# Layer statistics of a graph-attention stage moved into the feed-forward steps, with reordered hand-overs in the attention step

## What is computed

```python
# end of the first layer
h2 = _layernorm(hidden, g2, b2)
hidden = hidden + gelu(h2 @ Wf1 + bf1) @ Wf2 + bf2

# second layer: graph_attention with 8 heads, then with one
attn_in = layer_norm(x, g1, b1)
h = einsum('bnd,dhk->bhnk', attn_in, W.reshape(D, H, Dh))
s = einsum('bhnk,hk->bhn', h, a_src)
t = einsum('bhnk,hk->bhn', h, a_dst)
e = leaky_relu(s[:, :, :, None] + t[:, :, None, :], 0.2) + bias[:, None, :, :]
attn = einsum('bhij,bhjk->bhik', softmax(e, axis=-1), h) + x
```

## Time and profile before

| | |
|---|---|
| median of 3 runs | 1096.09 us (1095.07 to 1099.65) |
| profiled execution, its own time | 1097.07 us |
| its span in the trace | 1095.2 us |
| busy: PE, DVE, ACT, POOL | 1043.2, 799.9, 710.2, 405.0 us |
| mean granted clock of PE | 0.989 of full speed |

### The profile page before, as it was taken

How to read it: one execution, slowest core, us unless ns; L and a number is a source line. 1 busy time by engine, 2 the same in 40 slices (tenths; PEclk the granted TensorE clock), 3 DMA queues, 4 the chain that set the end, 5 groups by cost and what they waited for, 6 DMA issues and landing times.

```text
span 1095.2 us, 39179 instructions
## 1 busy us (share of the span) xinstructions
PE 1043.2 (95%) x15924; PEld 915.1 (84%) x15924; DVE 799.9 (73%) x1921; ACT 710.2 (65%) x1718; POOL 405.0 (37%) x642
## 2 busy tenths in 40 slices
PE   5999999999999989999999999999989999979997
PEld 5888888888888868889988998898878888868886
DVE  4577777777777777865656565655678989858996
ACT  2777767777767754555455545555678888847774
POOL 3531121121111104332113211312367888877773
PEclk9999999999999999999999999999989999988999
DMA  9221111221110002110011001110000100001222
GB/s 239 55 46 42 41 41 41 58 62 41 41 41 12 12 2 59 27 32 21 21 28 29 23 21 28 31 40 1 22 23 19 29 19 19 13 3 59 78 78 98
DMA packets 82476, 43.67 MB, mean 40 GB/s; under 512 B 42912, under 2 KB 77984, under 8 KB 82336
## 3 DMA queue, kind: packets, MB, share of 16 engines
q1 hardware_dynamic: 78016, 41.44, 13.9%
q10 hardware_dynamic: 4320, 0.28, 0.3%
HBM read 21.25 MB, written 12.58 MB: 31 GB/s over the span
## 4 chain that ended last, share of the span: by engine, by line
PE 83%; DVE 5%; issue 4%; POOL 3%; ACT 2%; SPq 1%; DMA 1%; POOLq 0%; DVEq 0%; ACTq 0%
PE BK L1344 8%; PE BK L1346 8%; PE BK L1345 8%; PE BK L1473 6%; PE BK L1447 5%; PE BK L1560 5%; PE BK L1561 5%; PE BK L1562 5%; PE BK L1459 4%; PE BK L1440 3%; PE BK L1360 3%; PE BK L1369 3%; PE BK L1607 3%; PE BK L1361 2%; PE BK L1362 2%
## 5 line engine op out<-in xcount | busy, mean ns | idle before, releaser
L1192 ACT ACTIVATE gf<-BK,bcol 128x512 f32<-128x512 f32 x128 | 88.2, 689 | 160.0 <-PE BK L1346 146.5
L965 POOL TENSOR_TENSOR ve<-mv,eps_l 128x4 f32<-128x4 f32 x64 | 18.2, 284 | 438.1 <-DVE mv L314 419.4
L1108 ACT ACTIVATE e_sb<-BK,nmx 128x128 f32<-128x128 f32 x512 | 142.1, 408 | 28.3 <-DVE nmx L501 28.3
L597 DVE TENSOR_TENSOR gl<-gf,gh 128x512 fp32r<-128x512 f32 x128 | 100.8, 790 | 68.4 <-ACT gh L1193 66.6
L1560 PE MATMUL BK<-wf_hi,gh 128*128 128x256 f32 x512 | 142.7, 279 | 1.8 <-DVE gl L597 1.8
L1561 PE MATMUL BK<-wf_hi,gl 128*128 128x256 f32 x512 | 141.8, 277 | 0.0
L1562 PE MATMUL BK<-wf_lo,gh 128*128 128x256 f32 x512 | 141.7, 277 | 0.0
L507 DVE TENSOR_TENSOR pt_sb<-BK,ft 128x512 f32<-128x512 f32 x128 | 85.2, 687 | 59.3 <-PE BK L1447 57.8
L1128 ACT ACTIVATE xn<-x_all,neg_mr,rstd 128x256 f32<-128x256 f32 (+1 forms) x188 | 103.6, 610 | 4.7 <-POOL neg_mr L974 4.4
L1344 PE MATMUL BK<-xh,wf_hi 128*128 128x512 f32 x256 | 99.9, 390 | 1.4 <-DVE xl L341 0.8
L1346 PE MATMUL BK<-xh,wf_lo 128*128 128x512 f32 x256 | 100.9, 394 | 0.0
(11 more groups left out here) (207 smaller groups left out, 2760.8 us busy)
## 6 DMA issues: line engine op xcount, KB each, us to landing
x_all<-in_x_dram SPq DMA_DIRECT2D x16, 512.0 KB, 4.7
out_dram<-y SPq DMA_DIRECT2D x16, 512.0 KB, 2.9
xn<-tb_ln SPq DMA_DIRECT2D x240, 32.0 KB, 1.9
adj_in<-in_adj_dram SPq DMA_DIRECT2D x64, 64.0 KB, 3.6
adj_kept<-adj_tr SPq DMA_DIRECT2D x16, 256.0 KB, 2.3
adj_in<-adj_kept SPq DMA_DIRECT2D x16, 256.0 KB, 2.6
s_wf<-in_L_gnn_Wf_dram SPq DMA_DIRECT2D x2, 1024.0 KB, 7.2
s_w<-in_L_gnn_W_dram SPq DMA_DIRECT2D x2, 256.0 KB, 2.9
```

The source lines that it names most:

```text
L597: dve.tensor_tensor(gl[:, f, :], gf[f % 2][:], gh[:, f, :].bitcast(F32), ALU.subtract).then_inc(b_gl, 1)
L1108: e = act.activation(e_sb[:, j, :], LE[:, r, q, :], ACT.Exp, bias=nmx[:, j:j + 1], scale=1.0)
```

## The change

Three things are moved.

1. The statistics of the multi-head stage's layer norm are no longer made in that stage. New tiles hold mean, reciprocal deviation and shift of all 64 graphs. In feed-forward step i (1 to 15) DVE makes the four bn_stats of chunk i-1 after `gl` 4 (`layer_stats`) and the aggregates after `gl` 5 (`layer_aggr`), and POOL makes deviation and shift (`layer_scale`). Chunk 15 follows in multi-head steps 0 and 1. `far_stats`, `aggr` and POOL's deviations remain in multi-head steps 13 to 15 and 14 to 15, for the single-head stage. The last feed-forward step's own statistics for chunks 0, 1 and 2 go.
2. On PE the values of graph 0 stand right after the row scores, ahead of `c_av` and of the second ratios.
3. On ACT `gt_out` and `row_exps` stand ahead of the two `c_out_copy`; on DVE `row_limits` stands after `c_scale` 4 and `c_recip` after it, ahead of `c_scale` 5.

The core of the diff; the new tiles, the semaphores and the new counts of the shared ones are left out:

```diff
@@ -312,6 +324,24 @@
+def layer_stats(i):
+    wait_for(dve, cs_mv, i * G)
+    for g in range(G):
+        dve.bn_stats(cs_raw[:, g, :], xs(i, g)).then_inc(cs_st, 1)
+
+def layer_aggr(i):
+    dve.wait_ge(cs_st, (i + 1) * G)
+    for g in range(G):
+        dve.bn_aggr(cs_mean[:, i * G + g, :], cs_raw[:, g, :]).then_inc(cs_mv, 1)
+
+def layer_normalise(i):
+    dve.wait_ge(cs_rs, i + 1)
+    dve.wait_ge(ln_t, (i + CC) * KT)
+    for g in range(G):
+        n = i * G + g
+        dve.tensor_scalar(xn[:, g, :], xs(i, g), cs_mean[:, n, 0:1], cs_rstd[:, n:n + 1],
+                          ALU.subtract, ALU.mult).then_inc(ln_xn, 1)
@@ -587,45 +617,37 @@
 def b_step(i, half, par):
     final = isinstance(i, int) and i == NC - 1
-    c = CC if final else CB + 1 if i == 0 else i + CB + 2
+    c = CB + 1 if i == 0 else i + CB + 2
     for f in range(FT):
-        if f == 1 and i != NC - 2:
+        if f == 1 and i < NC - 2:
             dve.wait_ge(ln_st, (c + 1) * G)
         if f == 6 and i == 0:
             dve.wait_ge(ln_st, (CB + 3) * G)
         dve.wait_ge(b_gh, i * FT + f + 1)
         dve.tensor_tensor(gl[:, f, :], gf[f % 2][:], gh[:, f, :].bitcast(F32), ALU.subtract).then_inc(b_gl, 1)
-        if f == 0:
-            dve.wait_ge(*((b_x, G) if final else (a_x, (i + 2) * G)))
+        if f == 0 and i < NC - 2:
+            dve.wait_ge(a_x, (i + 2) * G)
             for g in range(G):
-                if i != NC - 2:
-                    stats(c, c % NC, g)
-        if f == 1 and i != NC - 2:
+                stats(c, c % NC, g)
+        if f == 1 and i < NC - 2:
             aggr(c)
+        if f == 4 and i > 0:
+            dve.wait_ge(b_x, i * G)
+            layer_stats(i - 1)
+        if f == 5 and i > 0:
+            layer_aggr(i - 1)
         if final and f == 2:
             setup_constants()
-        if f == 3 and (i == 0 or final):
+        if f == 3 and i == 0:
             normalise(c, c % NC)
-            if i == 0:
-                block_turn(c)
+            block_turn(c)
+        if f == 3 and final:
+            layer_normalise(0)
         if f == 5 and i == 0:
             for g in range(G):
                 stats(CB + 2, 2, g)
         if f == 6 and i == 0:
             aggr(CB + 2)
-        if final and f == 5:
-            dve.wait_ge(b_x, 3 * G)
-            dve.wait_ge(ln_mv, (CC + 1) * G)
-            for g in range(G):
-                stats(CC + 1, 1, g)
-        if final and f == 6:
-            dve.wait_ge(ln_st, (CC + 2) * G)
-            dve.wait_ge(ln_xn, (CC + 1) * G)
-            aggr(CC + 1)
-        if final and f == 7:
-            dve.wait_ge(ln_mv, (CC + 2) * G)
-            for g in range(G):
-                stats(CC + 2, 2, g)
     if final:
         ln_lo(i + CB + 1)
     for g in range(G):
@@ -673,12 +695,9 @@
 def far_stats(i):
-    c = i + CC + 3
-    wraps = isinstance(i, int) and i >= NC - 3
-    nxt = i + 3 - NC if wraps else i + 3
-    dve.wait_ge(ln_mv, c * G)
-    if wraps:
-        dve.wait_ge(c_x, C_START + (nxt + 1) * G)
+    c, nxt = i + CC + 3, i + 3 - NC
+    dve.wait_ge(ln_mv, ln_count(c) * G)
+    dve.wait_ge(c_x, C_START + (nxt + 1) * G)
     for g in range(G):
         stats(c, nxt, g)
@@ -747,25 +766,32 @@
     if back:
         c_scale(i - 1, 2)
         c_scale(i - 1, 3)
-    dve.wait_ge(ln_st, (i + CC + 3) * G)
-    dve.wait_ge(ln_nm, nm_count(i + CC + 1, CC))
     if back:
         row_shifts(i)
-    aggr(i + CC + 2)
+    if isinstance(i, int) and i >= NC - 2:
+        c = i + CC + 2
+        dve.wait_ge(ln_st, ln_count(c + 1) * G)
+        if c > CD:
+            dve.wait_ge(ln_nm, nm_count(c - 1))
+        aggr(c)
+    if back:
+        c_scale(i - 1, 4)
+        row_limits(i, par)
     if back and not (isinstance(i, int) and i == 1):
         c_recip(i - 2, par)
     if back:
-        c_scale(i - 1, 4)
         c_scale(i - 1, 5)
-    if back:
-        row_limits(i, par)
-    if back:
         c_scale(i - 1, 6)
         c_scale(i - 1, 7)
     lo_part(i + 1, 1 - par)
     dve.wait_ge(c_bq, i + 1)
     hb_out(i, par, 0)
-    far_stats(i)
+    if isinstance(i, int) and i == 0:
+        layer_stats(NC - 1)
+    if isinstance(i, int) and i == 1:
+        layer_aggr(NC - 1)
+    if isinstance(i, int) and i >= NC - 3:
+        far_stats(i)
 chunks(dve, b_step)
 dve.wait_ge(b_x, NG)
 looped(dve, c1_step, tail=4)
@@ -961,18 +987,33 @@
+def layer_scale(i):
+
+    n = slice(i * G, (i + 1) * G)
+    pool.wait_ge(cs_mv, (i + 1) * G)
+    wait_for(pool, cs_nm, i)
+    pool.tensor_tensor(cs_tmp[:], cs_mean[:, n, 1], eps_l1[:], ALU.add).then_inc(cs_ve, 1)
+    pool.wait_ge(cs_ve, i + 1)
+    pool.tensor_tensor(cs_rstd[:, n], cs_tmp[:], neg_half[:], ALU.pow).then_inc(cs_rs, 1)
+    pool.wait_ge(cs_rs, i + 1)
+    pool.tensor_tensor(cs_tmp[:], cs_mean[:, n, 0], cs_rstd[:, n], ALU.mult).then_inc(cs_mr, 1)
+    pool.wait_ge(cs_mr, i + 1)
+    pool.tensor_tensor(cs_shift[:, n], zero_g[:], cs_tmp[:], ALU.subtract).then_inc(cs_nm, 1)
@@ -991,19 +1032,24 @@
         elif first == CC:
-            pool.wait_ge(ln_xn, (i + CC + 2) * G)
-            rstd_of(i + CC + 2, EPS[CC])
-            neg_mean_of(i + CC + 2, CC)
+            if isinstance(i, int) and i == 1:
+                layer_scale(NC - 1)
+            if isinstance(i, int) and i >= NC - 2:
+                pool.wait_ge(ln_xn, (i + CC + 2) * G)
+                rstd_of(i + CC + 2, EPS[CD])
+                neg_mean_of(i + CC + 2)
         elif first == CB:
-            for c in ((CB + 1, CB + 2) if i == 0 else () if i == NC - 2 else (CC,) if i == NC - 1 else (i + CB + 2,)):
+            for c in ((CB + 1, CB + 2) if i == 0 else () if i >= NC - 2 else (i + CB + 2,)):
                 pool.wait_ge(ln_xn, c * G)
-                rstd_of(c, EPS[CC if c == CC else CB])
+                rstd_of(c, EPS[CB])
+            if i > 0:
+                layer_scale(i - 1)
@@ -1122,8 +1165,14 @@
     else:
         nxt = i + 1
     c = i + first + 1
-    act.wait_ge(ln_nm, nm_count(c, first))
     act.wait_ge(ln_t, c * KT)
+    if first == CC and not (isinstance(i, int) and i == NC - 1):
+        act.wait_ge(cs_nm, NC if isinstance(i, int) and i == NC - 2 else NC - 1)
+        for g in graphs:
+            act.activation(xn[:, g, :], xs(nxt, g), ACT.Identity, scale=cs_rstd[:, bass.ds(nxt * G + g, 1)],
+                           bias=cs_shift[:, bass.ds(nxt * G + g, 1)]).then_inc(ln_xn, 1)
+        return
+    act.wait_ge(ln_nm, nm_count(c))
     for g in graphs:
         act.activation(xn[:, g, :], xs(nxt, g), ACT.Identity, scale=rstd[:, g:g + 1],
                        bias=neg_mr[:, g:g + 1]).then_inc(ln_xn, 1)
@@ -1216,12 +1265,12 @@
     if back:
         normalise(i, CC, range(G))
         far_minima(i)
+    if back:
+        gt_out(i, half, par)
+        row_exps(i)
     if back and not (isinstance(i, int) and i == 1):
         c_out_copy(i - 2, par, 1)
         c_out_copy(i - 2, par, 2)
-    if back:
-        gt_out(i, half, par)
-        row_exps(i)
     hi_part(i + 1, 1 - par)
     bq_out(i, par)
     inverse_rows(i, par, 0)
@@ -1639,12 +1688,12 @@
         pe.wait_ge(c_hb, i * 2)
         c_st(i, 0, par)
         c_st(i, 1, par)
+    c_h_out(0, par)
     if far:
         for h in range(4, H):
             c_av(i - 2, par, h)
     if back:
         ratios(i - 1, 1 - par, 1)
-    c_h_out(0, par)
     c_h_out(1, par)
     if back:
         c1_turn(i + 1)
```

More of the change, by code:

```diff
@@ L114, in build @@
         sb("region", [P, REGION // 4 + 8])
+        cs_raw = sb("cs_raw", [P, G, 6])
+        cs_mean = sb("cs_mean", [P, NG, 2])
+        cs_rstd = sb("cs_rstd", [P, NG])
+        cs_shift = sb("cs_shift", [P, NG])
+        cs_tmp = sb("cs_tmp", [P, G])
         def overlay(base, limit):
@@ L259, in build, with nm_count, ln_count @@
         EPS = {CA: eps_l0, CB: eps_l0, CC: eps_l1, CD: eps_l1}
-        def nm_count(c, first):
-            return c if first == CA else c - (CC - NC)
+        cs_st, cs_mv, cs_ve, cs_rs, cs_mr, cs_nm = (
+            sem(n) for n in ("cs_st", "cs_mv", "cs_ve", "cs_rs", "cs_mr", "cs_nm"))
+        def nm_count(c):
+            return c if c <= CB else c - CD + NC + 1
+        def ln_count(c):
+            return c if c < CC else c - NC
         def xs(i, g):
@@ L790, in c2_step @@
                 if ahead:
-                    dve.wait_ge(ln_nm, nm_count(i + CD + 1, CD))
-                    dve.wait_ge(ln_st, (i + CD + 3) * G)
+                    dve.wait_ge(ln_nm, nm_count(i + CD + 1))
+                    dve.wait_ge(ln_st, ln_count(i + CD + 3) * G)
                 if old:
@@ L797, in c2_step @@
                 if far:
-                    dve.wait_ge(ln_mv, (i + CD + 3) * G)
+                    dve.wait_ge(ln_mv, ln_count(i + CD + 3) * G)
                     stats(i + CD + 3, i + 3, 0)
@@ L963, in rstd_of, with neg_mean_of @@
             def rstd_of(c, eps):
-                pool.wait_ge(ln_mv, c * G + G)
+                n = ln_count(c)
+                pool.wait_ge(ln_mv, n * G + G)
```

(18 more changed lines are left out.)

2 lines of the change are left out of this document (1 added, 1 removed).

## The result

| | before | after |
|---|---|---|
| median of the runs | 1097.22 us (4 runs, 1095.07 to 1099.65) | 1121.61 us (4 runs, 1119.85 to 1125.72) |
| profiled execution | 1097.07 us | 1119.85 us |
| its span | 1095.2 us | 1117.7 us |

The changed kernel is slower by some 2%: the ratio of its time to that of the kernel before is 1.0215 (95% interval 1.019 to 1.0239). The profiled executions lie 22.8 us apart; the forecast was 17.2 us. First the table by stage. The columns are window, us, the busy time and count of PE, its weight loads, DVE, ACT and POOL, then PE's granted clock (1.00 is 2.4 GHz, 0.50 is 1.2 GHz), DMA share and GB/s.

What follows compares the result with a forecast made beforehand. Bound by a chain of hand-overs between PE, DVE and ACT. 13.0 + 0.5 - 0.7 + 4.4 = +17.2 us on 1097.07 gave 1114.3 us, as a median 1113 against 1096.09; range 1099 to 1125, about 8 in 10.

Steps and rivals of the forecast that it cites:

- the order's term: Multi-head steps 2 to 15: later transposes lengthen the period from 11.88 to 12.8 us, +13.0 us in 14 steps (9.8 to 15.4).
- the clock's: Multi-head steps: PE idle some 1.5 us halves its clock in 2 of 14 steps, 2.2 us each, +4.4 us (0 to 31).
- DVE's freed time counts 0: Steady multi-head step: the 1.9 us of statistics and aggregates taken off DVE turn into waiting, gain 0.
- The second ratios come 0.14 us later: Steady multi-head step: values of graph 0 fill PE's 0.59 us wait, ratios start 0.14 us later (0 to 0.25).
- c_scale 5 is 0.79 us later behind row_limits and the reciprocal: Steady multi-head step on DVE: row_limits (0.49 us) and reciprocal (0.3 us) delay c_scale 5; transposes come 0.93 us later.
- the clock falls in most steps: Rival for the multi-head steps: +13 us plus ten clock falls of 2.2 us, 1131 us in all; chance 7%.
- Step 1 of the multi-head stage: Ratios start no earlier and row_limits delays the transposes by 0.49 us: +0.5 us.
- The last feed-forward step: DVE drops statistics there, so PE's 0.98 us wait before the row scores shrinks: -0.7 us (0 to -0.98).
- POOL's new operations end before the next bias additions are needed: Feed-forward steps: POOL's added statistics operations end in time, the additions being needed some 20 us later: 0.
- The faster one: Rival: the 0.59 us wait before the second ratios goes and nothing replaces it, 9 us gained, 1087 us; chance 9%.
- no change: Rival: row_limits and reciprocal do not delay c_scale 5, only the reorder counts, +1.8 us, 1098 us; chance 9%.
- GpSimd's power operation beside gl: Feed-forward steps: forecast adds nothing for it; a rival had gl 7 0.3 us late, 5 us more, 1118 us; chance 3%.

Runs made afterwards that it cites:

- e3: Kernel before with only the layer-norm statistics moved, the multi-head orders of PE, ACT and DVE as before: 1099.73 us, ratio 1.0011.
- e2: Changed kernel with PE's order of before, the second ratios ahead of the values of graph 0: 1107.45 us, ratio 1.0067.
- e1: Changed kernel with c_scale 5 put back directly behind c_scale 4, ahead of row_limits and the reciprocal: 1097.87 us, ratio 0.9996.
- e9: Changed kernel with PE computing the values of graphs 0 and 1 twice, filling its wait before the transposes: 1108.65 us, ratio 1.0096.
- e12: Changed kernel with PE's old order, row minima behind the fourth value product, and in feed-forward step 1 layer_scale(0) behind w_lo: 1094.47 us, ratio 0.9969.
- e4: Kernel before with the statistics moved and PE's new order; ACT and DVE keep their multi-head orders of before: 1101.3 us, ratio 1.0024.

## Why the prediction was right, point by point

The direction, the mechanism and the place held; the median was 8.6 us over the forecast and inside the range. That it stayed inside is in part luck: the order's term came out some 3.5 us too high and the clock's some 7.9 us too low, and the one took from the other.

- **DVE's freed time counts 0.** Right. DVE waits 1.30 us ahead of c_scale 4 in the changed kernel, and e3 has the same stage, 186.42 us.
- **The second ratios come 0.14 us later.** They come 4.79 us after the first (818.88 to 823.67) in place of 4.75: 0.04, inside the bounds of 0 and 0.25.
- **c_scale 5 is 0.79 us later behind row_limits and the reciprocal.** From the second ratios to c_scale 4 it takes 1.33 us (foreseen 1.32); limits and reciprocal hold DVE for 0.43 us (825.61 to 826.04) and 0.27 us (826.04 to 826.31), 0.70 us in all in place of the sum's 0.49 and 0.3. Row_limits itself takes 0.48 us at its new place and took 0.57 at the old one; why, no run shows. Together the period became 12.57 us, not 12.8, and the order's term 14 x 0.68 = 9.5 us (12.56 us in e2, less 11.88), not 13.0: just under its lower bound of 9.8. e1 and e2 measured it.
- **The clock.** This is the term that was mis-sized: 4.4 us forecast, about 12.3 measured (the stage's 21.8 less 9.5; 10.1 by e9, 13.8 by e2). The forecast had two falls of 2.2 us; there were ten stretches at half clock of 3.41 us in the stage, one in step 1 and nine in the steps that follow, each of the nine lengthening its step by some 1.42 us (13.97 us, their mean, less 12.55). The price came from a stretch of 6.82 us, twice as long as these; the changed kernel has no stretch of that length in the stage, which takes 2.2 us off the sum. The number of falls was a guess from one idle time of 1.81 us that was followed by one and one of 2.07 us that was not. The rival "the clock falls in most steps" had the count right and the price too high.
- **Step 1 of the multi-head stage.** Its transposes come 0.35 us later than before, where 0.49 was foreseen. But the clock fell there too, and the step took 13.45 us in place of 11.76: 1.7 us more, not 0.5.
- **The feed-forward stage.** The last feed-forward step gained about what was said: the 0.98 us ahead of the first row scores are gone,

```profile
763.98 0.28 PE L1611 MATMUL BK<-wf_lo,gh 128*128 128x256 f32 x1
764.40 0.50 PE L1393 MATMUL BK<-xh,wst_hi 128*128 128x512 f32 x1
```

and steps 3 to 14 kept their pace of 21.89 us. But from PE's first matmul on gl of step 0 to that of step 3 it lost 1.5 us, which the prediction did not see, so that the stage ends where it did. The step that failed is "POOL's new operations end before the next bias additions are needed": true of those additions, but in step 1 POOL also has w_lo queued, and DVE's weight preparation runs beside it. PE then waited, which it does neither before nor in e12:

```profile
458.09 0.39 PE L1609 MATMUL BK<-wf_hi,gh 128*128 128x256 f32 x1 [1.25 <-DVE x_all L666]
```

- **The rivals.** The faster one needed c_scale 5 within 1.9 us of the second ratios. e1, with nothing between, has it done 2.6 us after them (864.87 to 867.49), as worked out, and gains nothing. The rival "no change" has the time of e1 and e4, where row_limits and the reciprocal were taken out of the way. GpSimd's power operation beside gl cost nothing: in the step of the earlier trace rows as it is now, gl 7 starts within it and takes 0.69 us:

```profile
605.78 0.69 DVE L627 TENSOR_TENSOR gl<-gf,gh 128x512 fp32r<-128x512 f32 x1 [0.66 <-ACT gh L1242]
```

```profile
605.27 1.01 POOL L1012 TENSOR_TENSOR cs_rstd<-cs_tmp,neg_half 128x4 f32<-128x4 f32 x1
```

## What to carry to other kernels

Where two engines hand work back and forth, filling one wait moves the loss to the next hand-over of the same cycle; before spending a reorder on it, write down when each wait of the cycle would end if the other were open, and take out what delays the producer (the row minima between two products) rather than what the consumer does meanwhile. An operation that is not late should not be moved ahead of one that another engine waits for, however little it takes. And in this kernel a wait on TensorE cost more than its length when it grew into one long piece: two waits of 0.56 and 0.68 us left the clock alone, one of 1.34 us mostly did not.
